# Where the receptance mix of a four-stage fused model is made, and when its gate sums begin

## The reference

```
x = x + L0(x)                 # causal conv, small state space, scan over T
x = x + LSTM(x)               # 512 steps; the result is "x2" below
# L2: mixture of experts by token hash, gated by a receptance
xprev = concat(cond, x[:, :-1])
xk = x + (xprev - x) * time_maa_k ;  xr = x + (xprev - x) * time_maa_r
expert_in = gather of xk by slot             # 16 experts, 512 tokens each
h = square(relu(expert_in @ w_key)) ; expert_out = h @ w_value
y = expert_out[slot] ; r = sigmoid(xr @ w_recept.T)
x = x + r * y
# L3: per feature and row: |x| -> softmax-like weights over T -> cumulative sum ->
#     index by a random value -> threshold -> x * (|x| >= threshold)
x = x + x * mask
```

## Time and profile before

| | |
|---|---|
| time, median of 3 (lowest to highest) | 4121.78 us (4120.27 to 4122.02) |
| the profiled execution: its time, its span | 4119.96 us, 4118.3 us |
| busy: PE, DVE, ACT, POOL | 94%, 74%, 41%, 7% of the span |
| recurrence | up to about 3003 us |
| experts | first load 3011.67 us, PE's last product 3774.58 us |
| finishing | from 3783.9 us to the end |
| matmul records of the sums (L1147) | 512, 231.6 us busy |
| DMA | 266.94 MB, mean 65 GB/s |

### The profile page before, as it was taken

How to read it: one execution, slowest core, us unless ns; L and a number is a source line. 1 busy time by engine, 2 the same in 40 slices (tenths; PEclk the granted TensorE clock), 3 DMA queues, 4 the chain that set the end, 5 groups by cost and what they waited for, 6 DMA issues and landing times. The chain is left out here.

```text
span 4118.3 us, 111735 instructions
## 1 busy us (share of the span) xinstructions
PE 3858.1 (94%) x44034; PEld 2530.6 (61%) x44034; DVE 3047.6 (74%) x9953; ACT 1677.9 (41%) x5296; POOL 292.5 (7%) x362
## 2 busy tenths in 40 slices
PE   3999999999999999999999999999769999997995
PEld 3566666666656666665666666666457888875442
DVE  9888888888878888887888888875545544552798
ACT  3334433333433333333333333433234434443675
POOL 1000000000000000000000000000000000001343
PEclk8999999999999999999999999999989999998998
DMA  7121111112111111211111112100043343333353
GB/s 287 28 37 27 27 35 27 31 31 37 27 28 27 35 27 32 38 29 28 27 35 27 32 30 37 27 17 15 12 166 123 130 157 141 122 112 123 123 184 112
DMA packets 387862, 266.94 MB, mean 65 GB/s; under 512 B 288953, under 2 KB 322233, under 8 KB 384292
## 3 DMA queue, kind: packets, MB, share of 16 engines
q1 hardware_dynamic: 365648, 184.21, 17.8%
q0 software_dynamic: 17696, 66.79, 4.2%
q10 hardware_dynamic: 4020, 9.10, 0.6%
HBM read 176.48 MB, written 83.92 MB: 63 GB/s over the span
## 5 line engine op out<-in xcount | busy, mean ns | idle before, releaser
L387 PE MATMUL bank<-buf,buf 128*16 128x256 f32 x32768 | 1872.3, 380 | 62.5 <-DVE buf L705 52.9
L387 PEld LDWEIGHTS bank<-buf,buf 128*16 128x16 f32 x32768 | 906.0, 97 | 883.1 <-DVE buf L705 78.9
L841 PE MATMUL bank<-buf,buf 128*128 128x256 f32 (+1 forms) x3072 | 1036.7, 337 | 2.7 <-DVE buf L1012 2.7
L842 PE MATMUL bank<-buf,buf 128*128 128x256 f32 (+1 forms) x3072 | 978.3, 318 | 0.0
L843 PE MATMUL bank<-buf,buf 128*128 128x256 f32 (+1 forms) x3072 | 977.4, 318 | 0.0
L599 DVE SCALAR_TENSOR_TENSOR buf<-buf,buf,buf 128x256 f32<-128x256 f32 x1920 | 870.6, 480 | 0.8 <-issue 0.8
L683 DVE STREAM_TRANSPOSE buf<-bank 128x256 f32<-128x256 f32 x1024 | 459.9, 449 | 449.4 <-PE bank L387 409.3
L556 ACT ACTIVATE buf<-buf 128x96 f32<-128x96 f32 x1024 | 290.4, 284 | 1136.6 <-DVE buf L688 1136.0
L841 PEld LDWEIGHTS bank<-buf,buf 128*128 128x128 f32 x3072 | 581.2, 189 | 253.3 <-issue 215.2
L843 PEld LDWEIGHTS bank<-buf,buf 128*128 128x128 f32 x3072 | 583.3, 190 | 41.3
L842 PEld LDWEIGHTS bank<-buf,buf 128*128 128x128 f32 x3072 | 584.2, 190 | 38.5
(11 more groups left out here) (139 smaller groups left out, 2906.5 us busy)
## 6 DMA issues: line engine op xcount, KB each, us to landing
buf<-in_wk SPq DMA_DIRECT2D x16, 2048.0 KB, 9.6
buf<-in_wv SPq DMA_DIRECT2D x16, 2048.0 KB, 9.3
buf<-in_xT SPq DMA_DIRECT2D x62, 496.0 KB, 3.8
buf<-in_xB SPq DMA_DIRECT2D x32, 512.0 KB, 3.6
expert_in_scratch<-buf POOLq DMA_DIRECT2D x16, 1024.0 KB, 22.6
x_scratch<-buf SPq DMA_DIRECT2D x32, 512.0 KB, 9.6
buf<-expert_in_scratch SPq DMA_DIRECT2D x16, 1024.0 KB, 11.6
expert_out_scratch<-buf POOLq DMA_DIRECT2D x64, 256.0 KB, 4.7
```

The costliest lines, as they stand in the source:

```text
L387: last = mm(gate_ps[hf][32 * j:32 * j + B, 0:HCOLS], hist[:, k, at_step(slot_at)], wh[:, k, j * GCOLS + hf * HCOLS:j * GCOLS + (hf + 1) * ...
L841: nc.tensor.matmul(out, left[0], right[0], start=first, stop=False)
L842: nc.tensor.matmul(out, left[0], right[1], start=False, stop=False)
```

## The change

The mix xr of batch row e is made in the experts' stage, beside expert e: SP loads x2 of row e with its halo column (`load_x2`), ACT weighs chunk a after it has copied out y piece a (`weigh_last`), DVE mixes after it has split w_key of the next expert (`mix_in`), and SP stores the mixed row to a new DRAM scratch `xr_scratch` (`store_mixed`) before it issues the next w_key load. `x2_scratch` gets one more column per row, in which the recurrence's first store also puts the halo; so the pieces of the other stores move by 4 bytes. A class `Gating` holds the buffers and semaphores that both phases use. They lie over buffers of the experts' stage that are free early in the last expert; there SP loads w_recept, the mixed rows 0 to 2 and x2 of rows 0 and 1, and after the last expert's product PE sums the receptance of rows 0 and 1 and ACT makes their gates, ahead of the barrier. In the finishing phase the mix, the weighing and the halo are gone; SP loads a mixed row beside each row of x2, into a ring of three.

```diff
-    x2_d = nc.dram_tensor("x2_scratch", (P, KD, B, T), F32, kind="Internal").ap()
+    x2_d = nc.dram_tensor("x2_scratch", (P, KD, B, 1 + T), F32, kind="Internal").ap()
+    xr_d = nc.dram_tensor("xr_scratch", (P, KD, B, T), F32, kind="Internal").ap()
...
+    def load_mixed(self, sp, xr_d, i):
+        if i >= self.XR_RING:
+            sp.wait_ge(self.s["r_summed"], KD * (i - self.XR_RING + 1))
+        sp.dma_start(self.xr[i % self.XR_RING], xr_d[:, :, i, :]).then_inc(self.xr_landed[i % self.XR_RING], 16)
...
 # expert_phase, SP, one(e)
                 sp.dma_start(wv_raw, ins["wv"][:, bass.ds(e * KF, KF), :]).then_inc(s["wv_landed"], 16)
+                if later(e, 1):
+                    sp.wait_ge(s["xr_made"], KD * e)
+                    store_mixed(e - 1)
+                else:
+                    sp.dma_start(maa_r, ins["maa_r"]).then_inc(s["maa_landed"], 16)
+                load_x2(e)
 
             experts(sp, one)
+            sp.wait_ge(s["turned"], KD * E)
+            sp.wait_ge(s["wk_ready"], KD * E)
+            sp.wait_ge(s["xr_stored"], 16 * (E - 1))
+            sp.dma_start(gating.wr, ins["wr"]).then_inc(gating.s["wr_landed"], 16)
+            for i in range(gating.XR_RING):
+                gating.load_mixed(sp, xr_d, i)
+            sp.wait_ge(s["h_summed"], KF * E)
+            for i in range(2):
+                gating.load(sp, x2_d, i)
+            sp.wait_ge(s["xr_made"], KD * E)
+            store_mixed(E - 1)
+            sp.wait_ge(s["xr_stored"], 16 * E)
...
 # expert_phase, PE and ACT after experts(...)
+            for i in range(2):
+                gating.receptance(pe, i)
...
+            for i in range(2):
+                gating.open_gate(act, i, 0, KD)
...
 # expert_phase, ACT after the copy of y piece a; DVE at the end of one(e)
+                    weigh_last(e, a)
...
+                for k in range(KD):
+                    mix_in(e, k)
...
 # finish_phase
-            receptance(0)
             turn(0)
-            receptance(1)
             turn(1)
-            receptance(2)
+            gating.receptance(pe, 2)
...
             for i in range(B):
                 scan(i)
                 bound(i)
                 if i + 1 < B:
                     combine(i + 1)
-                if i + 3 < B:
-                    mix_in(i + 3)
                 choose(i)
...
                 if i + 1 < B:
                     exponent(i + 1)
-                if i + 4 < B:
-                    weigh_last(i + 4)
```

More of the change, by code:

```diff
@@ L848, in expert_phase @@
+def expert_phase(nc, ctx, ins, carve, banks, keep, gating, x2_d, xr_d, rows_d, y_d):
     ident = keep["ident"]
@@ L850, in expert_phase @@
     TURN_FROM = 3
-    wk_raw, wv_raw = carve(KD, FF), carve(KF, D)
+    rows = [carve(NS, D) for _ in range(2)]
+    wk_raw = carve(KD, FF)
+    xT_hi, xT_lo = ([carve(KD, CAP, dt=F32R) for _ in range(2)] for _ in range(2))
     wk_hi, wk_lo = carve(KD, FF, dt=F32R), carve(KD, FF, dt=F32R)
+    assert carve.top == gating.top
+    wv_raw = carve(KF, D)
     wv_hi, wv_lo = carve(KF, D, dt=F32R), carve(KF, D, dt=F32R)
-    rows = [carve(NS, D) for _ in range(2)]
-    xT_hi, xT_lo = ([carve(KD, CAP, dt=F32R) for _ in range(2)] for _ in range(2))
+    x2_row, xr_row = carve(KD, 1 + T), carve(KD, T)
+    maa_r, maa_last, maa_now = carve(KD), carve(KD), carve(KD)
     relu = [carve(CAP) for _ in range(2)]
@@ L959, in _ @@
             experts(pe, one)
+            pe.wait_ge(s["xT_ready"], KD * E)
+            pe.wait_ge(gating.s["wr_landed"], 16)
+            for i in range(2):
+                gating.receptance(pe, i)
         @block.scalar
@@ L968, in split_wk, with weigh_last @@
                     nc.scalar.activation(wk_hi[:, k, :], wk_raw[:, k, :], ACT.Copy).then_inc(s["wk_hi_ready"], 1)
+            def weigh_last(e, k):
+                if k == 0:
+                    if not later(e, 1):
+                        act.wait_ge(s["share_ready"], 2)
+                    act.wait_ge(s["x2_landed"], 16 * (e + 1))
+                    if later(e, 1):
+                        act.wait_ge(s["xr_stored"], 16 * e)
+                nc.scalar.activation(xr_row[:, k, :], x2_row[:, k, 0:T], ACT.Copy, scale=maa_last[:, k:k + 1])\
+                    .then_inc(s["weighed"], 1)
             split_wk(0)
@@ L1017, in _ @@
             split_wk(0)
+            dve.wait_ge(s["maa_landed"], 16)
+            v.tensor_scalar(maa_last, maa_r, 0.5, None, ALU.mult).then_inc(s["share_ready"], 1)
+            v.tensor_scalar(maa_now, maa_r, -0.5, 0.5, ALU.mult, ALU.add).then_inc(s["share_ready"], 1)
+            dve.wait_ge(s["share_ready"], 2)
             def one(e, par):
@@ L1034, in one, with finish_phase @@
                     split_wk(e + 1)
+                for k in range(KD):
+                    mix_in(e, k)
             experts(dve, one)
-def finish_phase(nc, ctx, ins, carve, banks, keep, x2_d, y_d, out):
+def finish_phase(nc, ctx, ins, carve, banks, keep, gating, x2_d, xr_d, y_d, out):
     ident, cond, place = keep["ident"], keep["cond"], keep["place"]
[L1042 to L1048, removed]
+    RING, NC = gating.RING, T // P
+    stream, gate, landed = gating.stream, gating.gate, gating.landed
     rows = [[carve(D) for _ in range(NC)] for _ in range(2)]
@@ L1171, in _ @@
                 if i + 3 < B:
-                    receptance(i + 3)
+                    gating.receptance(pe, i + 3)
         @block.scalar
```

173 lines of the change are left out of this document (81 added, 92 removed).

## The result

The changed kernel takes 5832.6 us (median of 4 runs, 5821.6 to 5890.5) against 4121.0 (4120.2 to 4122.0): a ratio of 1.418, 95% interval 1.414 to 1.423. The forecast was 4088. It is wrong by 1745 us, and nearly all of that stands in the one paragraph of the prediction that ends "Cost nil": the recurrence.

What follows compares the result with a forecast made beforehand. DVE was taken to bound the finishing stage, PE the experts' stage. Beats 21.2 + start 13.1 - experts 0.5 = 33.8 us off the profiled 4119.96 gives 4086.2; with the median 1.8 above, forecast 4088, range 4080 to 4102.

Steps and rivals of the forecast that it cites:

- Cost nil: Recurrence: x2 stores shift by 4 bytes, only the last near a barrier; longest landing 18.4 us stays hidden; no cost.
- The fifth rival: Recurrence: shifted pieces make the last x2 store 2.5 times 9.2 us, moving the experts' block about 4: 4092; chance 0.04.
- The beat: Finishing stage, per row: falls from 17.27 to 15.5 us without DVE's mix-ins; twelve beats give 21.2 us.
- The start: Finishing stage up to scan 1: gates of row 1 made early bring scan 1 forward, 13.1 us gained.
- the 2.9 us for the low clock: Start: PE, back at a low clock after idling, needs 2.9 us more for half of row 2's sums.
- The experts' stage: Added mix-ins, weighings and transfers are covered, PE stays the bound; only 0.5 us for a wait in expert 0.
- The cover for ACT, DVE and w_key: Experts' stage: weighing and mix-in leave ACT and DVE 1.5 and 2.1 us to spare; w_key's queue needs 10.9 of 23.6.
- The prediction's own sign: Experts' stage: a length grown by over 5 us would show a step of the prediction wrong.
- Rivals 1 to 4: Start gives nothing, 4101 (0.12); PE and DVE collide, 4099 (0.14); w_key late, 4150 (0.05); early sums late, 4101 (0.03).

Runs made afterwards that it cites:

- e1: Kernel before, with the x2 scratch starting 4 bytes later and rows still 2048 B apart: 4442.65 us.
- e5: Kernel before, with x2 scratch rows of 513 floats, data beginning at the second one: 5895.94 us.
- e8: Computation left out, only stores of 8192 pieces of 64 B, by row pitch and start: 2052 B rows at 0 and 4 took 60 to 64 us.
- e9: Computation left out, only such 64 B stores, by row and partition spacing: 2052 B rows, partitions 139264 B apart, took 22.9 and 24.2 us.
- e2: Changed kernel with the x2 scratch laid out as before and the halo column in its own small scratch: 4091.88 us.
- e6: e1 with each tile's store cut in four, issued at different places of the tile: 4154.49 us.
- e7: e2 with the new buffers carved behind y, so that all others have the addresses of before: 4082.13 us.
- e10: e7 with the gate sums of rows 0 and 1 after the barrier, loads still early: 4082.75 us.
- e3: Kernel before, with only the changed kernel's order of buffers in the experts' stage: 4129.81 us.

## Why the prediction was wrong

Its steps one by one:

- **The recurrence, "Cost nil": this step failed.** The prediction put it: "The x2 stores shift by 4 bytes; only the last one is near a barrier", and took the longest landing of before, 18.4 us, as the bound. Both halves are wrong. The size: a landing of the old layout says nothing of one off the 32 B grid. Stores alone, at the change's spacing, took 60 to 102 us where a store landed in 9.6 before: the 4 bytes bring it to about 28 (e1), the spacing of rows and partitions does the rest (e5, e8, e9). The fifth rival had the shifted pieces, with a factor of 2.5 that no row stood behind, and priced one store, 4 us. The place: "near a barrier" counts only engines that wait for the store's data. 31 other stores that nobody waits for were taken as free. What was left out is that the 16 DMA engines carry the instruction packets too. The last store went out 1677 us later than before, 54 us for each of 31 tiles; the wait behind it took another 55.
- Two doses agree with that, as an estimate: at 9.6 us a store costs nothing; at about 28, 9.5 us a tile (e1's last store went out 295.5 us late); at 60 to 102, 54. With 15.7 us of code in hand, as the one tile above has it, these would be nil, 12, and 44 to 86. The layout as the cause is shown (e2 without it, e5 with nothing else). The inner mechanism is read from the trace (no packet of queue 8 for 39 us while PE stands) and fits e6, but e6 changed the DMA time as well. Which code packets wait behind which data packets, or whether they wait in the queues or at the DRAM, was not tried.
- **The beat, right.** 15.50 forecast as 15.5, with Abs as the wait of 0.71 us in DVE, and PE without a gap.
- **The start, right in sum, off in its reason.** In the changed kernel 13.7 gained for a forecast of 13.1, and there two misses cancel. The gathers landed later than reckoned (combine 0 at 45.1 us after the early sums began, forecast 42.5), and the 2.9 us for the low clock were not paid by the sums of row 2: they began at 50.3, ran 13.90 long, and the granted clock was 0.98 and then 1.00. The low clock fell on turn 0 (3.65 us for the usual 1.91). With the layouts mended (e7) the gathers came earlier, the sums of row 2 began at 46.6, and the gain is 83.2-64.4 = 18.8. And e10 shows that the prediction credited the wrong edit: the loads and mixes made beforehand give it, the early sums do not.
- **The experts' stage: not nil but 10 us.** The cover for ACT, DVE and w_key was there (no wait of ACT for w_key behind the first expert, though its landing went from 9.6 to 14.0). What was missed stood in the diff as an order of `carve` calls: e3 and e7 show it both ways. The prediction's own sign, a stage longer by over 5 us, was met.
- Rivals 1 to 4 didn't occur.

Without the one float the forecast would have been 4088 for a measured 4091.9 (e2). That is closer than its parts: the experts' 9 us that were missed and 4 us more gained at the start (16.9 for 13.1) partly cancel.

## What to carry to other kernels

Keep every piece of a DRAM store on the 32 B grid at both ends, pad rows to it, and keep a halo column out of a row that is stored in short pieces. A transfer for which nobody waits is not free: where engines run long code that is fetched as it runs, compare its length in the DMA queues with how much of it they have in hand (here 15.7 us). Cutting it up and spreading it out took away nine tenths of the loss in e6. When work is moved ahead of a barrier, ask what stands behind that barrier: here the early sums paid only once the gathers went with them.

## What the runs showed that was not expected

- Off the 32 B grid, 8192 stored pieces of 64 B, rows 2048 B apart, took 25 to 37 us and not 7.7, and 60 to 102 with partitions 131328 B apart and rows 2052 B apart; loads of 2 KB pieces at 4 B took 7.1 against 7.3.
- PE stood for 27.29 us between two matmuls of one sum, with no instruction packet for 39 us; during such a jam the granted clock fell to 0.52, and the last store was waited for 67.1 us.
- The same stores, cut in four and spread out, took all 16 DMA engines 405 us more than before and not 1114.
- Other SBUF addresses of operands took PE from 821 to 811 matmuls in 600 us, 9 us of the kernel's time, with no idle time in either.
